# Rows of q and k copied by 0/1 matrices on TensorE instead of through DRAM, and two q projections moved into the attention groups

## The chip, the cores and the metric

One core of a Trainium2 chip runs one launch of the kernel. The metric is device time in microseconds (us). TensorE is called PE here, VectorE DVE, ScalarE ACT, GpSimd POOL; SP is the engine that only issues transfers.

## The reference

```python
x  = hidden_states                       # (4, 1024, 128), float32
xn = (x - mean(x)) / sqrt(var(x) + 1e-5)
q  = (xn @ Wq.T + bq).reshape(b, t, 16, 8)      # 16 heads of 8
k  = (xn @ Wk.T + bk).reshape(b, t, 4, 8)       # 4 key/value heads
v  = (xn @ Wv.T + bv).reshape(b, t, 4, 8)
q, k = q*cos + rotate_half(q)*sin, k*cos + rotate_half(k)*sin
scores  = einsum('bthd,bshd->btsh', q, repeat(k, 4)) / sqrt(8)
context = einsum('btsh,bshd->bthd', softmax(scores, axis=2), repeat(v, 4))
ffn = (silu(xn @ wg.T) * (xn @ wu.T)) @ wd.T    # 384 hidden, weights int * 1/127
out = x + context @ Wo.T + bo + ffn
```

## The kernel before

**Groups.** The attention is done in NG = 16 groups, one for each pair of batch and key/value head; a group has G = 4 query heads of 8 rows. Group g belongs to batch g // 4. Every group needs its q and k in an unusual shape: each float32 number is split in three bfloat16 parts (high, middle, low), and the six products of parts that matter (BLOCKS) are laid under one another, so that one matmul over 48 rows gives a score in nearly float32. In SBUF this is `qa`, `ka` (48 rows for even heads at rows 0 to 47, for odd heads at 64 to 111) and a second copy with three more rows for the maxima, `qc`, `kc`. So the same 8 rows of `part` (the tile of the three parts, q and k by row) must stand at several places of the partition axis.

**How the rows get there.** `part` is written to the DRAM tensors `q_rows`, `k_rows` (`store_k`, `store_q`, and a loop on POOL for group 0's q), and read back at the rows wanted (`load_k`, `load_q`, `load_parts`).

**Head.** x is loaded, each batch gets its moments (`moments`, DVE), the root and a Newton step (`root`, on ACT and on DVE), its normalised form `xn` (`normalise` on DVE for batch 0, on POOL for 1 and 2, by ACT for 3), its transposes (`transpose_xn` on PE, `copy_xn_T` on ACT). Batch 0's first 96 rows of q and its 32 rows of k are projected, rotated (`rotate`) and split on DVE and ACT. Then follow 48 units (LEAD) of the first group's row maxima, which this text calls the ramp.

**A unit.** `max_unit` on PE multiplies 128 queries with 512 keys (L916), DVE takes the maximum of the bank (`reduce_max`, L762). In the ramp the units go round three PSUM banks, and other work of PE is placed behind units by number: transposes of batches 2, 3 (PE_XN), the rest of k and q of batch 0 (PE_S1), v (PE_V, PE_VT), q of batches 2 and 3 (PE_Q, eight matmuls). `ident16`, and the weights of the feed-forward layer (`w_ffn`, L756), are converted on DVE ahead of the ramp. When the ramp is through, PE waits for `raw_done`, `w_done` and `qc_loaded`, and does the first four score matmuls (L933).

**Steps.** A group has 16 steps. In a step PE does four max units for a part of the rows that lies 48 units ahead, four score matmuls of the next step, at most one other job between them (JOB_AT, OUT_AT), and last `weigh` (L1002), which multiplies the exponentials with v. ACT makes the exponentials (L590), DVE the maxima. The units and the jobs of a step go round four PSUM banks in the order that `step_order` writes out; PE waits (`bank_left`) until the bank four places earlier has been read. Jobs GATE, UP at steps 1 to 4, 6, 7, NEG_T at 5 and 13, CTX at 8 and 16, DOWN at 10 and 11. Steps 9, 12, 14 and 15 have none in groups 0 and 1. Seven later groups have STAGE at 9 and PROJ at 12 and 14. A score matmul waits for the exponential three units back (`score_before`). After GATE, ACT makes two copies of its bank; after UP one.

**Later batches.** `split_later(b)` on POOL rotates and splits q of batch b, in group b - 1; it is followed by the stores to `q_rows`. Batch 1's q is projected just ahead of the ramp.

Of the kernel before, what the change touches and what calls it, by code (L numbers as in the profile page):

```python
# [67 lines left out]
MAX, GATE, UP, DOWN, NEG_T, CTX, STAGE, PROJ = "max", "gate", "up", "down", "neg_T", "ctx", "stage", "proj"  # L68

# [4 lines left out]
MIDDLE = (GATE, UP, DOWN, PROJ)  # L74
# [13 lines left out]
OUT_AT[NG - 1] = output_steps(OUTS - 2)  # L88

# [46 lines left out]
def attention_swiglu(nc, x, wf, wi, biases, bo, tables, identity, out):  # L136
# [3 lines left out]
    with ExitStack() as ctx:  # L140
# [11 lines left out]
        ident16 = sb("ident16", [P, P], BF16)  # L152
# [71 lines left out]


# [28 lines left out]
        q_first = sem("q_first")  # L254
# [6 lines left out]
        id_done = sem("id_done")  # L261
# [64 lines left out]
        def _(sp):  # L326
# [92 lines left out]
        def _(pool):  # L419
# [8 lines left out]
            for n, made in enumerate((part_hi, part_mid, part_lo)):  # L428
                pool.wait_ge(made, 2)
                for i, (_, c) in enumerate(BLOCKS):  # L430
                    if c == n:
                        pool.dma_start(q_rows[0:1, :, i, :, :].rearrange("g j d t -> (g j) d t"),
                                       part[0:G * HD, 0, n, :]).then_inc(q_first, 16)
            pool.wait_ge(rstd_done, 3)
            normalise(pool, nc.gpsimd, 2, xn_done_pool)

            def split_later(i):
# [3 lines left out]
                pool.wait_ge(raw_done, 2 * PROJECTED.index(i) + 2)  # L441
# [97 lines left out]
        def _(act):  # L539
# [4 lines left out]
            act.dma_start(bo_sb[:, :], bo.partition_broadcast(P)).then_inc(const_in, 16)  # L544
            act.dma_start(wi_sb[:, :], wi).then_inc(ffn_in, 16)
# [50 lines left out]
            split_high(0)  # L596
            split_high(1)
            split_mid(0)
            split_mid(1)
            copy_xn_T(1)  # L600
            act.wait_ge(const_in, 48)
            copy_later(1, 0)
            root(slice(2 * NT, NTT), 2 * NTT + 3)
            nc.scalar.preload_act_table(ACT.Exp)
            copy_later(1, 1)
            act.wait_ge(rstd_done, 3)
            for t in range(NT):
                n = (B - 1) * NT + t
                last = nc.scalar.activation(xn[:, B - 1, t, :], y_all[:, n, :], ACT.Identity,
                                            bias=shift[:, n:n + 1], scale=rstd[:, n:n + 1])  # L610
            last.then_inc(xn_done_act, 1)
            for b in range(2, B):
                copy_xn_T(b)
            for n in range(2):
                copy_later(0, n)
# [598 lines left out]
```

## Time and profile before

| | |
|---|---|
| time, median of 3 runs (lowest, highest) | 770.75 us (769.08, 771.15) |
| time of the profiled execution | 768.65 us |
| its span, first to last instruction | 766.0 us |
| PE busy | 720.9 us, 94% |
| DVE busy | 688.1 us, 90% |
| ACT busy | 621.9 us, 81% |
| POOL busy | 222.9 us, 29% |

2.65 us of the profiled execution lie outside its span. The head takes the first 34 us, the ramp lasts to about 69 us, the 16 groups to about 757 us. A time in a row is counted from the start of the span. A busy PE is not a PE at its peak, for its matmuls overlap; so the text goes by the distance between the starts of instructions.

### The profile page before, as it was taken

Reading aid. Unit: us, or ns where it says so; the run is one execution under the profiler, and the core shown is the slowest. Engines: PE = TensorE matmul, PEld = TensorE weight load, DVE = VectorE, ACT = ScalarE, POOL = GpSimd, SP = SyncE. Lnnn points to the kernel's source line nnn. Section 1 sums busy time; section 2 is a strip of 40 time slices with the busy share of each in tenths; the row PEclk is TensorE's granted clock in tenths of the full one; section 3 lists DMA queues with packets and bytes.
Section 4 is the critical chain, followed back from the end, with each engine's and each line's share of the span. In section 5 each row is a group of like instructions: output and inputs, shape, how many; then the busy total and the mean of one; then the engine's idle time right before and its main releaser. Section 6 shows DMA issues by size and latency. Waiting matters only on the chain.

```text
span 766.0 us, 13616 instructions
## 1 busy us (share of the span) xinstructions
PE 720.9 (94%) x4856; PEld 211.8 (28%) x4856; DVE 688.1 (90%) x1286; ACT 621.9 (81%) x1277; POOL 222.9 (29%) x364
## 2 busy tenths in 40 slices
PE   3598999999999999999999999999999999999997
PEld 1222222222222222323222222323222222323232
DVE  7688999999999999999999999999999999999911
ACT  1535989888888988888888978888897979888895
POOL 3408656473830302112030302112030302103030
PEclk9789999999999999999999999999999999999999
DMA  6511124031321101011111101011111101110020
GB/s 222 138 38 32 57 60 129 19 114 34 85 62 33 33 1 49 16 32 33 33 32 32 33 1 44 21 33 33 34 32 32 33 2 34 31 32 2 2 84 27
DMA packets 29450, 34.35 MB, mean 45 GB/s; under 512 B 5672, under 2 KB 20264, under 8 KB 29256
## 3 DMA queue, kind: packets, MB, share of 16 engines
q1 hardware_dynamic: 26600, 26.23, 12.5%
q0 software_dynamic: 1920, 5.12, 2.2%
q10 hardware_dynamic: 864, 2.15, 0.8%
q8 instruction: 38, 0.62, 0.3%
q14 instruction: 28, 0.23, 0.1%
HBM read 23.12 MB, written 9.96 MB: 43 GB/s over the span
## 4 chain that ended last, share of the span: by engine, by line
PE 74%; DVE 16%; ACT 5%; issue 2%; DMA 2%; SPq 1%; ACTq 0%; DVEq 0%
PE acc_ps L1002 29%; PE banks L916 19%; DVE mx L762 13%; PE banks L933 10%; PE banks L1007 8%; ACT probs L590 4%; PE banks L1021 3%; PE banks L1013 2%; PE banks L886 1%; PE banks L892 1%; PE banks L1056 1%; DMA k_rows<-part 1%; DMA y_all<-in_x 1%; DVE y_all L809 1%; PE banks L1029 1%
## 5 line engine op out<-in xcount | busy, mean ns | idle before, releaser
L762 DVE TENSOR_REDUCE mx<-banks 128x1 f32<-128x512 f32 x1024 | 639.2, 684 | 34.6 <-PE banks L916 32.0
L590 ACT ACTIVATE probs<-banks 128x512 f32<-128x512 f32 x1024 | 550.6, 605 | 95.0 <-PE banks L933 89.8
L933 PE MATMUL banks<-qc,kc 51*128 51x512 bf16 x1024 | 307.2, 383 | 10.8 <-ACT probs L590 7.1
L916 PE MATMUL banks<-ka,qa 48*128 48x512 bf16 x1024 | 302.7, 385 | 11.7 <-DVE mx L762 6.3
L1002 PE MATMUL acc_ps<-probs,v_grp 128*32 128x512 f32 x2048 | 273.4, 606 | 0.0
L916 PEld LDWEIGHTS banks<-ka,qa 48*128 48x128 bf16 x1024 | 67.8, 94 | 300.2 <-DVE mx L762 234.8
L471 POOL TENSOR_TENSOR neg_max<-row_max,nought 128x16 bf16<-128x16 f32 x31 | 6.8, 220 | 294.5 <-DVE row_max L768 294.5
L933 PEld LDWEIGHTS banks<-qc,kc 51*128 51x128 bf16 x1024 | 66.2, 94 | 46.6 <-ACT probs L590 43.3
L1007 PE MATMUL banks<-xn_T,w_ffn 128*128 128x256 f32 x192 | 67.1, 431 | 0.0
L1002 PEld LDWEIGHTS acc_ps<-probs,v_grp 128*32 128x32 f32 x2048 | 40.4, 108 | 82.1 <-ACT probs L590 54.5
L515 POOL TENSOR_TENSOR gated<-gu 128x256 f32<-128x256 f32 x48 | 35.1, 732 | 51.9 <-ACT gu L647 51.9
L486 POOL COPY v_grp<-v_all 128x64 f32<-128x64 f32 x16 | 3.7, 236 | 134.0 <-PE acc_ps L1002 99.6
L1007 PEld LDWEIGHTS banks<-xn_T,w_ffn 128*128 128x128 f32 x192 | 28.5, 188 | 40.1 <-DVE mx L762 26.0
L518 POOL TENSOR_TENSOR th<-th,gated 128x256 f32<-128x256 f32 x48 | 34.9, 726 | 3.8
L520 POOL TENSOR_TENSOR hid<-th,gated 128x256 f32<-128x256 f32 x48 | 34.8, 725 | 3.8
L1013 PE MATMUL banks<-w_ffn,hid 128*128 128x128 f32 x192 | 29.9, 292 | 0.0
L1013 PEld LDWEIGHTS banks<-w_ffn,hid 128*128 128x128 f32 x192 | 23.8, 190 | 13.2 <-issue 6.8
L1021 PE MATMUL banks<-ident,acc_sb 128*128 128x128 f32 x124 | 19.4, 279 | 2.1 <-ACT acc_sb L659 0.6
L886 PE MATMUL banks<-xn_T,wf_sb 128*128 128x512 f32 x32 | 19.6, 732 | 1.2 <-ACT xn_T L555 1.2
L644 ACT ACTIVATE gu<-banks 128x256 f32<-128x256 f32 x48 | 19.3, 403 | 0.0
L659 ACT ACTIVATE acc_sb<-acc_ps 128x512 f32<-128x512 f32 x31 | 18.6, 599 | 0.6
L647 ACT ACTIVATE gu<-banks 128x256 f32<-128x256 f32 x48 | 18.8, 391 | 0.0
(94 smaller groups left out, 314.3 us busy)
## 6 DMA issues: line engine op xcount, KB each, us to landing
qa<-q_rows SPq DMA_DIRECT2D x32, 192.0 KB, 3.4
qc<-q_rows SPq DMA_DIRECT2D x64, 96.0 KB, 2.6
q_rows<-part POOLq DMA_DIRECT2D x18, 256.0 KB, 4.3
ka<-k_rows SPq DMA_DIRECT2D x32, 96.0 KB, 2.2
kc<-k_rows SPq DMA_DIRECT2D x32, 96.0 KB, 2.2
y_all<-in_x SPq DMA_DIRECT2D x4, 512.0 KB, 9.7
out<-y_all SPq DMA_DIRECT2D x16, 128.0 KB, 2.0
k_rows<-part SPq DMA_DIRECT2D x6, 192.0 KB
```

Source lines behind the costliest of these rows:

```text
L515: nc.gpsimd.tensor_tensor(gated[:, c, :], gu[:, c, 0:CH], gu[:, c, CH:2 * CH], ALU.mult).then_inc(gated_done, 1)
L518: nc.gpsimd.tensor_tensor(th[:, c, :], th[:, c, :], gated[:, c, :], ALU.mult).then_inc(gated_done, 1)
L520: nc.gpsimd.tensor_tensor(hid[:, c, :], th[:, c, :], gated[:, c, :], ALU.add).then_inc(hid_done, 1)
L590: nc.scalar.activation(probs[:, s % SLOTS, j, :], banks[:, score_bank(G * s + j), :], ACT.Exp, scale=SCALE).then_inc(exp_done, 1)
L762: nc.vector.tensor_reduce(out=mx[:, h, col, k:k + 1], in_=ps, op=ALU.max, axis=AX.X).then_inc(max_done, 1)
L886: return nc.tensor.matmul(s_ps[:, n, h, :], wf_sb[:, c + n * D:c + (n + 1) * D], xn_T[:, b * T + h * W:b * T + (h + 1) * W], start=True, s ...
L916: nc.tensor.matmul(ps, qa[par][rows, j // 2, t * P:(t + 1) * P], ka[par][rows, k * W:(k + 1) * W], start=True, stop=True).then_inc(a_ready, 1)
L933: nc.tensor.matmul(banks[:, score_bank(u), :], kc[par][rows, kt * P:(kt + 1) * P], qc[par][rows, h, j // 2, :], start=True, stop=True).the ...
L1002: last = nc.tensor.matmul(acc_ps[VC * j:VC * (j + 1), :], v_grp[par][:, kt, :], probs[:, s % SLOTS, j, :], start=(kt == 0), stop=(kt == NT ...
L1007: nc.tensor.matmul(ps[:, 0:CH], w_ffn[:, n * HID + c * P:n * HID + (c + 1) * P], xn_T[:, g * CH:(g + 1) * CH], start=True, stop=True).then ...
L1013: last = nc.tensor.matmul(ps[:, 0:D], hid[:, c, t * P:(t + 1) * P], w_ffn[:, 2 * HID + c * D:2 * HID + (c + 1) * D], start=(c == 0), stop= ...
L1021: last = nc.tensor.transpose(ps[:, t * P:(t + 1) * P], acc_sb[:, h, t * P:(t + 1) * P], ident[:, :])
```

## The change

Group 0's `ka` and `qa` are no longer loaded from DRAM. A new input `select` holds seven 128x128 bfloat16 matrices, six of zeros and ones and the identity (it takes the place of `ident16`). For each half of the 1024 tokens `replicate` multiplies three of them per part (k, q of heads 0 and 1, q of heads 2 and 3) with the 32 rows of `part`, three parts added up in PSUM, and ACT copies six banks into `ka[0]` and `qa[0]` (`copy_rows`). `kc[0]` and `qc[0]` are then copied from those by six transfers inside SBUF. Other heads' rows go through DRAM as before, by SP alone.

The order of the head changes with it. On DVE `root` of batch 1 moves behind the rotation, the moments of batches 2 and 3 come between and behind the splits, `root` of batches 2 and 3 moves behind the first unit's maximum, and the conversion of `w_ffn` moves ahead of the maximum of unit 46. POOL normalises batches 1 and 3, ACT batch 2.

The projection of batch 1's q moves from ahead of the ramp into it (PE_Q, four matmuls), and that of batches 2 and 3 to steps 9, 12, 14 and 15 of groups 0 and 1: each such job, LATER_Q, is one matmul of 512 columns in float32 and one copy of its bank by ACT (`project_later`).

```diff
-PROJECTED = (1, 0, 2, 3)
-assert len(PROJECTED) == B
-PE_XN, PE_S1, PE_V, PE_VT, PE_Q = (3, 5, 7, 9), (11, 13, 15, 17), (19, 21), (23, 24), tuple(range(26, 42, 2))
+PROJECTED = (0, 1)
+PE_XN, PE_S1, PE_V, PE_VT, PE_Q = (8, 10, 12, 14), (16, 18, 20, 22), (24, 26), (28, 29), (31, 35, 37, 39)
...
+for g in range(B - 2):
+    OUT_AT[g] = {9: (LATER_Q, 0), 12: (LATER_Q, 1), 14: (LATER_Q, 2), 15: (LATER_Q, 3)}
...
+        def select_bank(i):
+            return banks[:, (6, 4, 5, 1, 2, 3)[i], :]
...
-                store_k(slice(0, KV), slice(Q_ROWS, P), 0, n, k_stored[0])
+                store_k(slice(1, KV), slice(Q_ROWS + HD, P), 0, n, k_stored[0])
+                store_q(slice(1, KV - 1), slice(G * HD, Q_ROWS), 0, n, q_stored_too[0])
+            sp.wait_ge(ones_set, 4)
+            sp.wait_ge(select_done, 2 * PARTS)
+            for e in range(2):
+                rows = slice(e * E_ROWS, e * E_ROWS + MAX_ROW)
+                sp.dma_start(kc[0][rows, :], ka[0][rows, :]).then_inc(qc_loaded[0], 16)
+                for h in range(NH):
+                    sp.dma_start(qc[0][rows, h, :, :], qa[0][rows, :, h * W:(h + 1) * W]).then_inc(qc_loaded[0], 16)
             sp.wait_ge(k_stored[0], BLOCK_DMAS)
-            load_k(0, ka[0], qa_loaded[0])
-            sp.wait_ge(q_first, BLOCK_DMAS)
-            load_q(0, qa[0], qa_loaded[0])
-            sp.wait_ge(ones_set, 4)
-            load_parts(0, qc[0], kc[0], qc_loaded[0])
-            for n in range(PARTS):
-                store_q(slice(1, KV - 1), slice(G * HD, Q_ROWS), 0, n, q_stored_too[0])
...
-            for n, made in enumerate((part_hi, part_mid, part_lo)):
-                pool.wait_ge(made, 2)
-                for i, (_, c) in enumerate(BLOCKS):
-                    if c == n:
-                        pool.dma_start(q_rows[0:1, :, i, :, :].rearrange("g j d t -> (g j) d t"),
-                                       part[0:G * HD, 0, n, :]).then_inc(q_first, 16)
             pool.wait_ge(rstd_done, 3)
-            normalise(pool, nc.gpsimd, 2, xn_done_pool)
+            normalise(pool, nc.gpsimd, B - 1, xn_done_pool)
...
+                    pool.wait_ge(raw_later, 2 * NH * (i - 1))
...
+            act.dma_start(select_sb[:, :], select.bitcast(BF16)).then_inc(select_in, 16)
...
+            def copy_rows(i, rows):
+                act.wait_ge(select_ps, i + 1)
+                nc.scalar.activation(rows, select_bank(i), ACT.Copy).then_inc(select_done, 1)
+            def project_later(b, i, ps):
+                n, h = divmod(i, NH)
+                act.wait_ge(q_ps, 2 * len(PROJECTED) + 2 * NH * (b - 2) + i + 1)
+                nc.scalar.activation(raw[b][:, n, HALF[h]], ps, ACT.Identity,
+                                     bias=bias_sb[:, B_Q + n:B_Q + n + 1]).then_inc(raw_later, 1)
...
+            split_mid(0)
+            copy_rows(0, ka[0][:, HALF[0]])
             split_high(1)
-            split_mid(0)
+            copy_rows(1, qa[0][:, 0, HALF[0]])
             split_mid(1)
+            copy_rows(2, qa[0][:, 1, HALF[0]])
+            copy_rows(3, ka[0][:, HALF[1]])
+            for i in range(PAIRS):
+                copy_rows(4 + i, qa[0][:, i, HALF[1]])
             copy_xn_T(1)
-            act.wait_ge(const_in, 48)
-            copy_later(1, 0)
             root(slice(2 * NT, NTT), 2 * NTT + 3)
             nc.scalar.preload_act_table(ACT.Exp)
-            copy_later(1, 1)
             act.wait_ge(rstd_done, 3)
             for t in range(NT):
-                n = (B - 1) * NT + t
-                last = nc.scalar.activation(xn[:, B - 1, t, :], y_all[:, n, :], ACT.Identity,
+                n = 2 * NT + t
...
-            for i in PROJECTED[2:]:
-                for n in range(2):
-                    if (i, n) == (PROJECTED[-1], 0):
-                        copy_neg(0, 0, first_bank(NEG_BEHIND + 1))
-                    copy_later(i, n)
+            copy_neg(0, 0, first_bank(NEG_BEHIND + 1))
+            for n in range(2):
+                copy_later(1, n)
...
-            root(slice(NT, 2 * NT), 1)
...
+            rotate(0, 0)
+            rotate(0, 1)
+            rope_half(0)
+            rotate(1, 0)
+            rest_of_high(0)
+            rotate(1, 1)
+            low(0)
+            rope_half(1)
+            root(slice(NT, 2 * NT), 1)
+            rest_of_high(1)
+            moments(2, 4 * NT + 2)
+            low(1)
+            moments(3, 6 * NT + 2)
             add_eps(slice(2 * NT, NTT), 2 * NTT + 2)
-            root(slice(2 * NT, NTT), 2)
-            nc.vector.tensor_copy(ident16[:, :], ident[:, :]).then_inc(id_done, 1)
-            dve.wait_ge(ffn_in, 16)
-            for n, scale in ((slice(0, 2 * HID), DEQUANT), (slice(2 * HID, 3 * HID), 0.5 * DEQUANT)):
-                nc.vector.tensor_scalar(w_ffn[:, n], wi_sb[:, n], scale, None, ALU.mult).then_inc(w_done, 1)
             def reduce_max(g, a, ps):
                 dve.wait_ge(a_ready, AU * g + a + 1)
@@ -794,6 +828,12 @@
                 made.then_inc(neg_step, 1)
             for a in range(LEAD):
+                if a == 1:
+                    root(slice(2 * NT, NTT), 2)
+                if a == LEAD - 2:
+                    dve.wait_ge(ffn_in, 16)
+                    for n, scale in ((slice(0, 2 * HID), DEQUANT), (slice(2 * HID, 3 * HID), 0.5 * DEQUANT)):
...
+            def replicate(h, n, made):
+                pe.wait_ge(made, h + 1)
+                k_rows, q_rows = slice(Q_ROWS, P), slice(0, G * HD)
+                for i, (rows, a) in enumerate(((k_rows, 0), (q_rows, 0), (q_rows, 1))):
+                    c = (PARTS * a + n) * P
+                    last = nc.tensor.matmul(select_bank(3 * h + i), select_sb[rows, c:c + P], part[rows, 0, n, HALF[h]],
+                                            start=(n == 0), stop=(n == PARTS - 1))
+                    if n == PARTS - 1:
+                        last.then_inc(select_ps, 1)
+            pe.wait_ge(select_in, 16)
+            for h in range(2):
+                if h == 1:
+                    pe.wait_ge(rope_mul, 2 * NH)
+                for n, made in enumerate((part_hi, part_mid, part_lo)):
+                    replicate(h, n, made)
             for h in range(2):
                 transpose_xn(1, h)
-            pe.wait_ge(xnt_done, 4)
-            for n in range(2):
-                pe.wait_ge(rope_mul, 3 + n)
-                for h in range(2):
-                    last = project(C_Q, 1, n, h)
-                last.then_inc(q_ps, 1)
...
-            pe.wait_ge(qa_loaded[0], DMAS)
             for a in range(LEAD):
+                if a in (0, 2, 4):
+                    pe.wait_ge(select_done, 2 + a // 2)
...
-                    b, n, h = 2 + PE_Q.index(a) // 4, PE_Q.index(a) // 2 % 2, PE_Q.index(a) % 2
-                    if h == 0:
-                        if b > 2:
-                            pe.wait_ge(raw_done, 2 * (b - 1) + n + 1)
-                        elif n == 1:
-                            pe.wait_ge(v_done, 1)
-                    last = project(C_Q, b, n, h)
+                    n, h = divmod(PE_Q.index(a), NH)
+                    if n == 1 and h == 0:
+                        pe.wait_ge(v_done, 1)
+                    last = project(C_Q, 1, n, h)
...
+            def project_later(b, i, ps):
+                n, h = divmod(i, NH)
+                nc.tensor.matmul(ps, wf_sb[:, C_Q + n * D:C_Q + (n + 1) * D],
+                                 xn_T[:, b * T + h * W:b * T + (h + 1) * W], start=True, stop=True).then_inc(q_ps, 1)
...
+    for i, parts in enumerate(BLOCKS):
+        for e, d in itertools.product(range(2), range(HD)):
+            column = e * E_ROWS + i * HD + d
+            select[Q_ROWS + d, parts[0], column] = one
+            for pair in range(PAIRS):
+                select[(2 * pair + e) * HD + d, PARTS * pair + parts[1], column] = one
```

## Rows read from the trace of the kernel before

**Rows 1.** Chain that ended last, in order of time: start us, length us, what.

```profile
23.61 4.71 DMA k_rows<-part
...
29.68 3.60 DMA qa<-q_rows
```

**Rows 2.** Timeline of the head: start us, length us, engine, line, what, idle before.

```profile
15.51 4.92 POOL L315 TENSOR_SCALAR xn<-y_all,rstd,shift 128x128 f32<-128x128 f32 x8 [10.82 <-DVE shift L714]
...
16.83 0.69 DVE L737 TENSOR_TENSOR ctx_all<-probs 128x512 f32<-128x512 f32 x1
...
17.55 0.63 ACT L560 ACTIVATE part<-ctx_all 128x512 bf16<-128x512 f32 x1 [3.40 <-DVE ctx_all L737]
...
19.51 0.68 DVE L742 TENSOR_TENSOR ctx_all<-ctx_all,part 128x512 f32<-128x512 f32 x1
...
22.42 1.64 DVE L691 BATCH_NORM_STATS2 stats<-y_all 128x6 f32<-128x128 f32 x8
...
24.66 1.61 DVE L691 BATCH_NORM_STATS2 stats<-y_all 128x6 f32<-128x128 f32 x8
...
27.66 0.25 DVE L704 RECIPROCAL rc<-sd 128x16 f32<-128x16 f32 x1 [0.50 <-ACT sd L550]
...
29.01 0.82 DVE L756 TENSOR_SCALAR w_ffn<-wi_sb 128x768 f32<-128x768 int32 x2
...
29.07 4.00 POOL L315 TENSOR_SCALAR xn<-y_all,rstd,shift 128x128 f32<-128x128 f32 x8 [4.83 <-DVE shift L714]
```

**Rows 3.** Timeline of the ramp, same columns.

```profile
33.97 2.48 DVE L762 TENSOR_REDUCE mx<-banks 128x1 f32<-128x512 f32 x4 [4.14 <-PE banks L916]
...
35.25 1.12 PE L880 MATMUL banks<-ident,xn 128*128 128x128 f32 x4
...
40.12 1.29 DVE L762 TENSOR_REDUCE mx<-banks 128x1 f32<-128x512 f32 x2 [0.30 <-PE banks L916]
...
43.81 7.88 DVE L762 TENSOR_REDUCE mx<-banks 128x1 f32<-128x512 f32 x12 [0.82 <-PE banks L916]
...
53.09 1.12 PE L886 MATMUL banks<-xn_T,wf_sb 128*128 128x512 f32 x2
...
53.20 4.83 DVE L762 TENSOR_REDUCE mx<-banks 128x1 f32<-128x512 f32 x7 [0.21 <-PE banks L916]
...
61.73 8.41 DVE L762 TENSOR_REDUCE mx<-banks 128x1 f32<-128x512 f32 x13 [0.66 <-PE banks L916]
...
68.62 0.60 PE L933 MATMUL banks<-qc,kc 51*128 51x512 bf16 x3
```

**Rows 4.** Windows of time, all engines; the clock column is the last but two.

```profile
40.00:42.00 2.00, 1.85 (x12) 1.00 (x14) 1.58 (x3) 0.78 (x2) 0.00 (x0) 0.50 0.65 154
...
44.00:48.00 4.00, 4.00 (x34) 0.76 (x30) 3.91 (x7) 1.64 (x2) 0.00 (x0) 1.00 0.02 4
```

**Rows 5.** Timeline of PE, the matmuls that end steps 2, 3, 8, 9, 11 to 15 of group 0.

```profile
78.47 1.06 PE L1002 MATMUL acc_ps<-probs,v_grp 128*32 128x512 f32 x8
81.18 1.06 PE L1002 MATMUL acc_ps<-probs,v_grp 128*32 128x512 f32 x8
...
94.53 1.06 PE L1002 MATMUL acc_ps<-probs,v_grp 128*32 128x512 f32 x8
97.02 1.07 PE L1002 MATMUL acc_ps<-probs,v_grp 128*32 128x512 f32 x8
...
102.90 1.06 PE L1002 MATMUL acc_ps<-probs,v_grp 128*32 128x512 f32 x8
105.38 1.06 PE L1002 MATMUL acc_ps<-probs,v_grp 128*32 128x512 f32 x8
107.87 1.07 PE L1002 MATMUL acc_ps<-probs,v_grp 128*32 128x512 f32 x8
110.84 1.06 PE L1002 MATMUL acc_ps<-probs,v_grp 128*32 128x512 f32 x8
113.33 1.07 PE L1002 MATMUL acc_ps<-probs,v_grp 128*32 128x512 f32 x8
```

More of the change, by code:

```diff
@@ L1 @@
+import itertools
 from contextlib import ExitStack
@@ L72 @@
           10: (DOWN, 0), 11: (DOWN, 1), 13: (NEG_T, 0), 16: (CTX, 1)}
-MIDDLE = (GATE, UP, DOWN, PROJ)
+MIDDLE = (GATE, UP, DOWN, PROJ, LATER_Q)
 OUTS = 2 * B
@@ L133, in score_before, with attention_swiglu @@
     return max(v for v in range(-SG, u) if score_bank(v % SG) == score_bank(u))
-def attention_swiglu(nc, x, wf, wi, biases, bo, tables, identity, out):
+def attention_swiglu(nc, x, wf, wi, biases, bo, tables, identity, select, out):
     q_rows = nc.dram_tensor("q_rows", (NG, G, len(BLOCKS), HD, T), BF16, kind="Internal").ap()
@@ L260, in attention_swiglu @@
         w_done = sem("w_done")
-        id_done = sem("id_done")
+        select_in = sem("select_in")
+        select_ps = sem("select_ps")
+        select_done = sem("select_done")
         bo_added = sem("bo_added")
@@ L440, in split_later @@
                 rows, twin = (raw[i][:, k, :] for k in range(2))
-                pool.wait_ge(raw_done, 2 * PROJECTED.index(i) + 2)
+                if i in PROJECTED:
+                    pool.wait_ge(raw_done, 2 * i + 2)
+                else:
+                    pool.wait_ge(raw_later, 2 * NH * (i - 1))
                 nc.gpsimd.tensor_tensor(rows, rows, rope[:, 0, :], ALU.mult).then_inc(q_step, 1)
@@ L648, in group @@
                                                  ACT.Copy).then_inc(gu_done, 1)
+                        if kind == LATER_Q:
+                            project_later(g + 2, n, bank(slot))
                         if kind == NEG_T:
@@ L730, in _, with rope_half @@
             add_eps(slice(NT, 2 * NT), 4 * NT + 1)
-            root(slice(NT, 2 * NT), 1)
             dve.wait_ge(const_in, 48)
-            for h in range(2):
-                rotate(h, 0)
-                rotate(h, 1)
+            def rope_half(h):
                 dve.wait_ge(rope_mul, 2 * (h + 1))
@@ L738, in _, with rest_of_high @@
                     .then_inc(rope_sum, 1)
-            for h in range(2):
+            def rest_of_high(h):
                 dve.wait_ge(rope_sum, h + 1)
@@ L743, in _, with low @@
                                         ALU.subtract).then_inc(part_res, 1)
-            for h in range(2):
+            def low(h):
                 dve.wait_ge(part_res, h + 1)
@@ L748, in _ @@
                                         ALU.subtract).then_inc(part_lo, 1)
-            for b in range(2, B):
-                moments(b, 2 * b * NT + 2)
-            add_eps(slice(2 * NT, NTT), 2 * NTT + 2)
-            root(slice(2 * NT, NTT), 2)
-            nc.vector.tensor_copy(ident16[:, :], ident[:, :]).then_inc(id_done, 1)
-            dve.wait_ge(ffn_in, 16)
-            for n, scale in ((slice(0, 2 * HID), DEQUANT), (slice(2 * HID, 3 * HID), 0.5 * DEQUANT)):
-                nc.vector.tensor_scalar(w_ffn[:, n], wi_sb[:, n], scale, None, ALU.mult).then_inc(w_done, 1)
+            rotate(0, 0)
[11 more added lines that the diff above has]
+            moments(3, 6 * NT + 2)
+            add_eps(slice(2 * NT, NTT), 2 * NTT + 2)
             def reduce_max(g, a, ps):
@@ L876, in transpose_xn @@
                     pe.wait_ge(xnt_done, 2 * b + h - 1)
-                if b == 2 and h == 0:
-                    pe.wait_ge(raw_done, 1)
                 for t in range(HT):
@@ L901, in _ @@
                     project(C_S0, 0, n, h).then_inc(proj_ps, 1)
+            def replicate(h, n, made):
[13 more added lines that the diff above has]
+                    replicate(h, n, made)
             for h in range(2):
                 transpose_xn(1, h)
-            pe.wait_ge(xnt_done, 4)
-            for n in range(2):
-                pe.wait_ge(rope_mul, 3 + n)
-                for h in range(2):
-                    last = project(C_Q, 1, n, h)
-                last.then_inc(q_ps, 1)
             def max_unit(par, a, ps):
@@ L1069, in bank_left @@
                     pe.wait_ge(y_done, CT * g + n + 1)
+                elif kind == LATER_Q:
+                    pe.wait_ge(raw_later, 2 * NH * g + n + 1)
                 elif kind == NEG_T:
@@ L1098, in take @@
                     ffn_down_proj(g, n, ps)
+                elif kind == LATER_Q:
+                    project_later(g + 2, n, ps)
                 elif kind == NEG_T:
@@ L1168, in _ @@
                 group(g, g // 2, g % 2, min(3, NG - g))
-_INS = ["x", "wf", "wi", "biases", "bo", "tables", "identity"]
+_INS = ["x", "wf", "wi", "biases", "bo", "tables", "identity", "select"]
 def kernel(**inputs):
@@ L1201 @@
     tables = np.stack([cos, sin], axis=1).astype(np.float32)
+    one = np.uint16(0x3F80)
+    select = np.zeros((P, PAIRS * PARTS + 1, P), dtype=np.uint16)
+    for i, parts in enumerate(BLOCKS):
[4 more added lines that the diff above has]
+                select[(2 * pair + e) * HD + d, PARTS * pair + parts[1], column] = one
+    select[range(P), PAIRS * PARTS, range(P)] = one
     arrays = {
@@ L1205 @@
         "identity": np.eye(P, dtype=np.float32),
+        "select": select.reshape(P, -1),
     }
```

30 lines of the change are left out of this document (17 added, 13 removed).

## The prediction

> **What bounds the kernel now.** I read the chain that ended last first. In the head it runs through two transfers, the store of k's parts to DRAM and the load of q from it [rows 1]; these the change takes off. Behind them it goes through PE, DVE and ACT by turns, with no transfer. Next the timeline of the head, for what stands ready when the transfers are gone; of the ramp, for what paces a unit; of PE in one group, for what a step costs with and without a job; and the windows, for the clock.
>
> The head: the first maximum begins at 33.97 after 4.14 us of idle DVE [rows 3]. So up to 4.1 us of pure waiting are to be had, and more only if DVE's work ahead of it shrinks.
>
> The ramp: alone, units come every 0.62 us (2.48 for 4); with a q projection behind every second one, every 0.69 us (4.83 for 7) [rows 3]. PE sets that pace, so each projection costs 2 x 0.07 = 0.14 us.
>
> A step: a step with no job (9, 12) takes 2.49 us, one with GATE or UP (3) 2.71 [rows 5]. In the latter PE is the limit. In the former it isn't: the fourth score matmul waits for the first exponential, and four maxima at 0.62 take 2.49 as well.
>
> **The head, worked out.** The first half's rotated rows stand at 16.83 + 0.69 = 17.52 as before [rows 2]. DVE then does, in the new order, a `rotate` of about 0.7 (18.2), `rest_of_high(0)` 0.68 (18.9; ACT's high part is ready, 17.55 + 0.63), `rotate` (19.6), `low(0)` (20.3), `rope_half(1)` (21.0) and `root` of batch 1. The like `root` took from 27.66 to just before the conversion at 29.01, with a small cast in it [rows 2]: 1.2 for its six instructions, so 22.2. From there three lines run:
> - DVE: `rest_of_high(1)` 22.9; moments of batch 2, 2.24 (22.42 to 24.66 [rows 2]), 25.15; `low(1)` 25.85; moments of batch 3, 28.1; eps 28.3.
> - POOL: `xn` of batch 1, 4.00 to 4.92 [rows 2], so 26.2 to 27.2. PE's eight transposes follow in two bursts of 1.12 that overlap a little [rows 3]: 28.1 to 29.1. Before, this root came at 14 and POOL began at 15.51; this is what is late next.
> - PE and ACT: the 18 select matmuls (512 columns each) are nowhere in the trace. Bounds: nothing, hidden behind DVE's splits, or, at the low clock, three of 0.43 each behind the last split. The last three banks can be copied from 25.85 + 0.6 = 26.5, 0.6 each (ACT's 512 columns take 0.63 [rows 2]): 28.4. Then two copies of `xn_T` behind the transposes to 29.7, and the square root to 29.9.
>
> So PE does unit 0 at 28.1 to 29.1 and DVE begins it at 28.7 to 29.6, 5 us earlier than now. But behind it stands `root` of batches 2 and 3, 1.2 us, which waits for ACT's square root: it ends at 31.1 to 31.5. I take 31.4 for the start of unit 1's maximum, against 33.97 + 0.62 = 34.6: **-3.2**. A dozen hand-overs between engines, at some 0.05 each, could add 0.6.
>
> **The ramp.** Four q projections instead of eight: 4 x 0.14 = **-0.55** (bounds 0 and -0.6). The other bursts are the same ones, five units later, and batches 2 and 3 stand normalised by 31.5 + 4 = 35.5, about when unit 8 is due. At the end the conversion of `w_ffn`, 0.82 [rows 2], which lay in the idle time ahead of the ramp, stands ahead of unit 46's maximum, and PE waits for it before the first scores. Now: unit 47's maximum ends at 61.73 + 8.41 = 70.14, so unit 44's at 68.2, and the scores start 0.4 later, at 68.62 [rows 3]. After: unit 44's ends at 68.2 - 3.2 - 0.55 = 64.45, unit 45's at 65.1, the conversion at 65.9, scores at about 65.95. That is **-2.65** for everything behind. In SP's queue twelve stores, six copies inside SBUF and group 1's loads stand ahead; from 22.2 on they have 40 us until the scores need `qc`, and so cost nothing; with no such cover each would add its issue. POOL loses six issues ahead of the second normalisation, which waits for `root` anyway. The `select` load has from about 4 to 18 us.
>
> **The moved projections.** Eight jobs of 512 columns, against 256 for GATE. In float32 such a matmul stands as two records; for 512 columns the two last 1.12 with the latency at their end [rows 3], of which 0.85 are streaming (1024 columns at two cycles each and 2.4 GHz). GATE's 256 columns stream for half of that, so the longer job adds 0.43 to a step like GATE's: LATER_Q step = 2.71 + 0.43, about 3.13. The bounds are the row's whole 1.12 on top of a step of 2.49, with no slack used (3.61, excluded as far as GATE's step shows that slack is used), and 3.13. ACT's copy of 0.6 is hidden: GATE steps carry two copies. The ring: four more slots per group, a multiple of its four banks, so nothing else changes its bank.
> - Step 9: 97.02 - 94.53 = 2.49 becomes 3.13, +0.64. Step 12 (102.90 to 105.38) +0.65. Step 15 (110.84 to 113.33) +0.64.
> - Step 13 (2.49): DVE has caught up in step 12, so it may give back up to 0.16.
> - Step 14 is 2.97 already (107.87 to 110.84), as the last score matmul of a group waits for the second exponential, not the first. The job lies in that wait: +0.16.
>
> Sum 1.9 to 2.1 per group, for two groups **+4.0** (bounds +3.2, if twice as much comes back, and +4.6, if step 14 pays in full as well).
>
> **Sum.** 766.0 - 2.65 + 4.0 = 767.35 span, 770.0 with the 2.65 outside it. The profiled execution lay 2.1 below the median of the runs, so the median goes from 770.75 to **772.1**, +0.17%. About 0.3% (2.3 us) is what a measurement of this kernel can tell from no change.
>
> **Rivals.**
> - *The clock (ends slower).* PE ran at the low level, 1.2 GHz, from the ramp's start to 42 and at 2.4 GHz from 44 [rows 4]; there the first burst of L892 left DVE idle for 0.82 and each of the transposes' four for about 0.3 [rows 3]. Now eight bare units come first and the bursts five units later, in sparser work. If the low level lasts through the three other bursts of PE_S1, each costs 0.82: +2.5, so 774.6. It decides from two bursts on (772.1 + 1.6 = 773.7). Against: the bursts themselves are the same that brought the clock up before. The Trainium skill ("TensorE: Matmul & The Clock Gate", Part 1, What's actually happening) says that the array's default is the throttled state and activity releases it; by that rule the sparser start is for this rival, and the row at 40 to 42 agrees.
> - *The head gives more (ends faster).* If unit 1's maximum waits for nothing but DVE's queue (28.3, unit 0, 1.2 of root: 30.1), the clock is high in the ramp (those gaps, 0.82 and four of 0.3, are gone) and the moved jobs cost their lower bound: 772.1 - 1.3 - 2.0 - 0.8 = 768.0. The one mechanism is the clock again, the other way: select matmuls and transposes directly ahead of the ramp, where PE now idles. It decides if it takes both the gaps and at least one us of the head.
> - *The jobs hide.* The steps of no job have slack of 0.42 each on PE; if the ring carried it over whole groups, 4 x 0.42 and step 14's wait would pay for more and the jobs would cost 1.0 less per group: 770.1, no change. Against: the ring is four banks deep, not a step.
> - *The head gives less.* If `xn` of batch 1 or the hand-overs cost 1.5 more, 773.6, slower.
>
> **Chances.** Forecast 0.40 (own range 770.8 to 773.4), clock 0.20, head less 0.13, head more 0.15, jobs hide 0.12. From these: faster by over 0.3% 0.15, within it 0.50 (part of the forecast's own spread passes the bound), slower 0.35. Range 768.9 to 775.0: it reaches to the clock's rival and to where the faster one begins.
>
> **What would show it.** First max unit at 28 to 29, `root` between the maxima of units 0 and 1, unit 1's maximum near 31.4; first scores near 66; a PE wait for `w_ffn` ahead of them; steps 9, 12, 15 of groups 0 and 1 at 3.13, step 14 at 3.1; group 2 on as before, the whole later by 1.3. Wrong would be: jobs of under 0.4 us, bursts of L892 with gaps of 0.8 after 45, or a first unit after 30.

## The result, and the profile after

In the runs made together, six of each kernel, before had a median of 769.3 us and the changed kernel 775.33 (772.21 to 778.73). The ratio is 1.0075, with a 95% interval from 1.0057 to 1.0093: slower by 0.75%, where 772.1 and no change that can be told were forecast, and above the range, which ended at 775.0.

The profiled execution shown here is the slowest of the six, 778.73 us with a span of 776.9. So its figures overstate the median's loss: 10.9 us of span against before's 766.0, where the medians lie 6.0 apart. First the head and the ramp, in the timeline (start, length, engine, line, what, idle before):

```profile
22.20 4.34 POOL L329 TENSOR_SCALAR xn<-y_all,rstd,shift 128x128 f32<-128x128 f32 x8 [17.51 <-DVE shift L741]
...
28.71 1.03 PE L965 MATMUL banks<-ka,qa 48*128 48x512 bf16 x3
...
29.35 0.69 DVE L796 TENSOR_REDUCE mx<-banks 128x1 f32<-128x512 f32 x1 [1.12 <-PE banks L965]
...
31.17 4.87 DVE L796 TENSOR_REDUCE mx<-banks 128x1 f32<-128x512 f32 x8
...
43.41 7.88 DVE L796 TENSOR_REDUCE mx<-banks 128x1 f32<-128x512 f32 x12 [0.84 <-PE banks L965]
...
57.13 2.07 PE L924 MATMUL banks<-xn_T,wf_sb 128*128 128x512 f32 x2
...
59.78 1.29 DVE L796 TENSOR_REDUCE mx<-banks 128x1 f32<-128x512 f32 x2 [1.85 <-PE banks L965]
...
62.33 1.29 DVE L796 TENSOR_REDUCE mx<-banks 128x1 f32<-128x512 f32 x2 [1.26 <-PE banks L965]
...
66.97 2.12 POOL L470 TENSOR_TENSOR part<-raw,part 128x1024 bf16<-128x1024 f32 x1
67.74 4.19 DVE L836 TENSOR_SCALAR w_ffn<-wi_sb 128x768 f32<-128x768 int32 x2
69.17 4.95 POOL L509 TENSOR_TENSOR y_all<-y_all,bo_sb 128x1024 f32<-128x1024 f32 x2
71.84 1.28 DVE L796 TENSOR_REDUCE mx<-banks 128x1 f32<-128x512 f32 x2
...
72.03 1.01 PE L982 MATMUL banks<-qc,kc 51*128 51x512 bf16 x3 [4.14 <-DVE w_ffn L836]
```

The head came as worked out. `xn` of batch 1 took 4.34, unit 0 was multiplied at 28.71, the maximum of unit 1 began at 31.17 (31.4 was forecast), 3.4 us ahead of before [rows 3]. Then the lead is lost. Two things stand out: the conversion of `w_ffn` takes 4.19 us instead of 0.82 [rows 2], while POOL works before it, beside it and behind it, and PE stands idle for 4.14 until it is done; and the q projections at 57.13 last 2.07 instead of the 1.12 of [rows 3], with DVE idle for 1.85 and 1.26. The first scores start at 72.03, 3.4 late against 68.62 and 6.1 after the forecast.

The windows of the same execution, whose third column from the end is the granted clock:

```profile
44.00:56.00 12.00, 9.46 (x62) 2.64 (x59) 10.66 (x22) 4.61 (x5) 0.98 (x3) 1.00 0.00 0
56.00:64.00 8.00, 7.79 (x15) 2.01 (x15) 4.41 (x7) 1.31 (x3) 7.78 (x5) 0.57 0.25 75
64.00:72.00 8.00, 2.68 (x8) 0.48 (x6) 7.86 (x9) 0.94 (x1) 7.78 (x5) 0.66 0.00 1
72.00:84.00 12.00, 11.63 (x44) 2.37 (x44) 6.91 (x12) 7.38 (x16) 6.74 (x3) 0.52 0.01 2
```

Before had 1.00, 1.00, 0.90 and 0.93 in these four. Now the clock is at its low level, 1.2 GHz, for most of 56 to 84. From 44 to 56 PE is busy for 9.46 us instead of 11.09, from 64 to 72 for 2.68 instead of 6.42.

What PE did just before the clock fell stands in its timeline. One matmul of a unit lasts 0.39 at the high level and 0.60 at the low one:

```profile
55.49 0.23 PE L970 MATMUL banks<-select_sb,neg_max 128*96 128x128 bf16 x1 [1.35 <-DVE neg_max L827]
56.00 0.39 PE L965 MATMUL banks<-ka,qa 48*128 48x512 bf16 x1 [0.28 <-DVE mx L796]
56.60 0.60 PE L965 MATMUL banks<-ka,qa 48*128 48x512 bf16 x1 [0.21 <-DVE mx L796]
...
66.68 1.20 PE L965 MATMUL banks<-ka,qa 48*128 48x512 bf16 x2 [0.21 <-DVE mx L796]
```

The first fall, between the units at 56.00 and 56.60, comes behind a wait of 1.35 us for the maxima that PE has to transpose (`neg_max`), with bare units (units with no other work of PE behind them) on its other side. The second is there by 66.68, behind bare units and ahead of the conversion (67.74): PE's long stop did not cause that fall, it lies inside the low stretch. Before has the same wait for `neg_max`, shorter and with a q projection directly behind the next unit, and its clock stays high there:

```profile
59.43 0.23 PE L921 MATMUL banks<-ident,neg_max 128*96 128x128 bf16 x1 [0.76 <-DVE neg_max L793]
59.94 0.39 PE L916 MATMUL banks<-ka,qa 48*128 48x512 bf16 x1 [0.28 <-DVE mx L762]
60.25 1.12 PE L886 MATMUL banks<-xn_T,wf_sb 128*128 128x512 f32 x2
```

Last comes PE's timeline at the ends of steps 0 to 2, 8, 9 and 11 to 15 of group 0, as in [rows 5]:

```profile
75.38 1.94 PE L1047 MATMUL acc_ps<-probs,v_grp 128*32 128x512 f32 x8
80.76 1.94 PE L1047 MATMUL acc_ps<-probs,v_grp 128*32 128x512 f32 x8
84.77 1.07 PE L1047 MATMUL acc_ps<-probs,v_grp 128*32 128x512 f32 x8
...
100.83 1.07 PE L1047 MATMUL acc_ps<-probs,v_grp 128*32 128x512 f32 x8
103.96 1.06 PE L1047 MATMUL acc_ps<-probs,v_grp 128*32 128x512 f32 x8
...
109.84 1.06 PE L1047 MATMUL acc_ps<-probs,v_grp 128*32 128x512 f32 x8
112.97 1.06 PE L1047 MATMUL acc_ps<-probs,v_grp 128*32 128x512 f32 x8
115.46 1.06 PE L1047 MATMUL acc_ps<-probs,v_grp 128*32 128x512 f32 x8
118.59 1.07 PE L1047 MATMUL acc_ps<-probs,v_grp 128*32 128x512 f32 x8
121.79 1.07 PE L1047 MATMUL acc_ps<-probs,v_grp 128*32 128x512 f32 x8
```

Step 9 takes 3.13, step 12 3.13, step 13 2.49, step 14 3.13 and step 15 3.20: 0.64, 0.65, 0, 0.16 and 0.71 more than in [rows 5], 2.16 in the group.

The budget of this execution against before's: 3.4 us later at the first scores, 6.3 at the end of step 2 (84.77 against 78.47), still 6.3 at the end of step 8, 8.5 behind step 15, 2.16 more in group 1, 0.3 elsewhere; 10.9 in all.

The six runs of the changed kernel say how much of this varies. From the longest to the shortest, with the mean granted clock of each:

```
778.73 us  0.971
776.24 us  0.975
775.82 us  0.976
774.84 us  0.978
773.92 us  0.978
772.21 us  0.980
```

A faster run never has a lower clock. From 0.980 to 0.971 is 0.009 x 777 x 2 = 14 us more at the low level, and 6.5 us more time.

### The profile page after: what moved, and what is told of

Its sections match the earlier page's. It is cut to its first block, busy times and chain, and to the rows that moved or that the text cites. A ratio compares the mean times of both kernels' runs of the same rounds, so it can differ in the third digit from the quotient of the medians.

```text
span 776.9 us, 13656 instructions
## 1 busy us (share of the span) xinstructions
PE 731.5 (94%) x4874; PEld 212.1 (27%) x4874; DVE 692.2 (89%) x1285; ACT 626.1 (81%) x1287; POOL 218.5 (28%) x358
## 4 chain that ended last, share of the span: by engine, by line
PE 78%; DVE 15%; ACT 4%; issue 2%; DMA 1%; SPq 0%; ACTq 0%; DVEq 0%
PE acc_ps L1047 29%; PE banks L965 20%; DVE mx L796 12%; PE banks L982 11%; PE banks L1057 8%; ACT probs L613 3%; PE banks L1071 3%; PE banks L1063 2%; PE banks L924 1%; PE banks L1053 1%; PE banks L930 1%; PE banks L1106 1%; DMA y_all<-in_x 1%; PE banks L918 1%; DVE w_ffn L836 1%
## 5 line engine op out<-in xcount | busy, mean ns | idle before, releaser
L965 PE MATMUL banks<-ka,qa 48*128 48x512 bf16 x1024 | 308.2, 389 | 8.2 <-DVE mx L796 8.2
L667 ACT ACTIVATE th<-banks 128x256 f32<-128x256 f32 x48 | 18.8, 392 | 0.8 <-PE banks L1057 0.8
```

Of the source, the lines that this page charges most:

```text
L965: nc.tensor.matmul(ps, qa[par][rows, j // 2, t * P:(t + 1) * P], ka[par][rows, k * W:(k + 1) * W], start=True, stop=True).then_inc(a_ready, 1)
```

## The experiments

Two theories stood to be tested. **P**: an instruction of DVE that converts from SBUF to SBUF stands still while POOL has an instruction running, and at unit 46 POOL does. **C**: the sparser ramp and PE's stop let the clock fall, and the bursts (the projections behind a unit) and first steps then run at the low level. Rivals: **L**, the conversion is slow for itself in that place; **W**, the clock only goes with waits that would be there anyway. Each ratio is to the kernel before, run in turn on the same chip; the changed kernel's is 1.0075.

**conv10.** The conversion ahead of unit 10's maximum.

```diff
-                if a == LEAD - 2:
+                if a == 10:
                     dve.wait_ge(ffn_in, 16)
```

> The changed kernel with one piece moved: the conversion of w_ffn on DVE stands ahead of unit 10's maximum instead of unit 46's, where POOL is idle. Theory P (the conversion took 4.19 us at unit 46 because an instruction of POOL was running, and PE stood still behind it for 4.14 us, which also let the clock fall): the conversion takes about 0.82 again, the first scores start near 67.5 instead of 72.03, and the low clock of 17 us around there shrinks to some 3 to 7 us. Time 5 to 8 us below the changed kernel's 775.3, so 767.5 to 770.5. Theory L (the conversion is slow for itself wherever it stands in the ramp): it still takes 4 us, now in front of unit 10, and the time stays within 2 us of 775.

Measured: 772.7, ratio 1.0034 (1.0017 to 1.0051), better than the changed kernel's 1.0075, whose interval begins at 1.0057, just above this one's end. The conversion in DVE's timeline:

```profile
36.10 0.82 DVE L836 TENSOR_SCALAR w_ffn<-wi_sb 128x768 f32<-128x768 int32 x2
```

0.82, so L falls. The first scores start at 65.48 in this execution; 1.0 us of that lead stands already at the first maximum (28.32 against 29.35), which the edit does not touch. But the clock was still 0.67 in the window from 56 to 64 and 0.57 in the next, and the gaps of 1.85 and 1.26 are still there: moving the conversion does not mend the clock in the ramp. The gain is 2.6 us by medians, 3.2 by ratios, where 5 to 8 were expected.

**poolheld.** The conversion stays at unit 46, POOL waits for it.

```diff
                 pool.wait_ge(q_step, n + 5)
+                if i == 0:
+                    pool.wait_ge(w_done, 2)
                 nc.gpsimd.tensor_copy(part[:, slot, 1, :], twin).then_inc(q_step, 1)
```

> The changed kernel with one wait more: POOL holds the last two instructions of the split of batch 0's q, and what follows, until w_ffn is converted; the conversion stays at unit 46. Theory P: with POOL idle the conversion takes 0.82 us instead of 4.19, the first scores start near 68.6, 3.4 us earlier than 72.03, and the low clock behind it is shorter; time 771 or less. Theory L: the conversion takes about 4.2 us as before and the time stays near 775.

Measured: 772.27, ratio 1.0043 (1.0021 to 1.0066). DVE's and POOL's timelines:

```profile
68.11 0.82 DVE L838 TENSOR_SCALAR w_ffn<-wi_sb 128x768 f32<-128x768 int32 x2
```

```profile
63.93 2.12 POOL L466 TENSOR_TENSOR raw<-raw,part 128x1024 f32<-128x1024 f32 x1
69.06 1.04 POOL L470 CAST part<-raw 128x1024 bf16<-128x1024 f32 x1 [3.02 <-DVE w_ffn L838]
```

In the same place, with POOL idle, it takes 0.82. This settles what P says of the duration. The time is less sure: 3.1 us better by medians, but the interval overlaps the changed kernel's (from 1.0057), and the median misses the 771 expected. In this execution PE's wait ahead of the scores is down to 0.77, and the clock is still low, 0.69 from 64 to 72 and 0.64 from 72 to 84.

**before_conv46.** The kernel before, with the conversion at unit 46 (the same lines, moved).

> The kernel before with one piece moved: the conversion of w_ffn from ahead of the ramp to ahead of unit 46's maximum. Theory P: POOL works there in this kernel too, so the conversion's two instructions take 2.5 to 4.5 us, PE waits for them before the first scores, and the clock falls for longer than the 3.4 us of before: 773 to 777 against 769.3. Theory L's variant (the delay belongs to the other changes of the head): 0.8 us and at most 771.

Measured: 773.16, ratio 1.005 (1.0031 to 1.0069). The two timelines:

```profile
71.14 2.40 DVE L797 TENSOR_SCALAR w_ffn<-wi_sb 128x768 f32<-128x768 int32 x2
```

```profile
69.89 2.12 POOL L454 TENSOR_TENSOR raw<-raw,part 128x1024 f32<-128x1024 f32 x1
72.07 1.25 POOL L456 CAST part<-raw 128x1024 bf16<-128x1024 f32 x1
```

2.40, with ends that go with POOL's: the first of its two instructions lasts 1.29 instead of 0.55 and ends 0.41 behind POOL's first row, the second lasts 1.19 instead of 0.35 and ends 0.21 behind POOL's cast, which itself takes 1.25 instead of 1.04. One misplaced instruction pair alone makes the kernel before 0.5% slower (four runs), more than its own 1.6 us; the rest was not taken apart.

**before_laterq.** The kernel before with the moved projections of batches 2 and 3 alone.

```diff
-PROJECTED = (1, 0, 2, 3)
+PROJECTED = (1, 0)
...
-PE_XN, PE_S1, PE_V, PE_VT, PE_Q = (3, 5, 7, 9), (11, 13, 15, 17), (19, 21), (23, 24), tuple(range(26, 42, 2))
+PE_XN, PE_S1, PE_V, PE_VT, PE_Q = (3, 5, 7, 9), (11, 13, 15, 17), (19, 21), (23, 24), ()
...
+for g in range(B - 2):
+    OUT_AT[g] = {9: (LATER_Q, 0), 12: (LATER_Q, 1), 14: (LATER_Q, 2), 15: (LATER_Q, 3)}
```

> The kernel before with q of batches 2 and 3 projected at steps 9, 12, 14, 15 of groups 0 and 1 alone (the ramp then holds no q projection). The step theory: each of the two groups is longer by 2.16 us (0.64, 0.65, 0.16, 0.71), the ramp shorter by 8 x 0.14 = 1.1. If that is all: 769.3 + 4.3 - 1.1 = 772.5. Theory C (the bursts of the ramp also kept the clock up): without them the low level returns before unit 47 and lasts into the first steps, 2 to 4 us more: 774.5 to 776.5.

Measured: 773.42, ratio 1.0056 (1.004 to 1.0071). Its windows:

```profile
56.00:64.00 8.00, 6.09 (x13) 1.17 (x12) 7.42 (x17) 0.27 (x1) 4.18 (x2) 0.50 0.08 20
64.00:72.00 8.00, 7.66 (x22) 1.66 (x25) 6.87 (x12) 2.89 (x7) 7.63 (x6) 0.50 0.20 56
```

Without the q bursts the clock is low from 56 to 72, and the weigh of step 0 takes 1.94. The steps cost what they cost in the change (98.53 - 95.40 = 3.13 for step 9). Without the clock 772.5 was expected, with it 774.5 to 776.5: the time lies between, so it decides for neither, and what shows the clock's part here is the windows (before had 1.00 and 0.90).

**conv10_fill.** conv10 with 16 idle matmuls on PE (their result is read by nobody), 13 behind units and three ahead of the wait for `neg_max`.

```diff
+FILL = (30, 32, 33, 34, 36) + tuple(range(40, 48))
...
+            def fill(n):
+                for _ in range(n):
+                    nc.tensor.matmul(acc_ps[:, :], select_sb[:, 0:P], select_sb[:, 0:W], start=True, stop=True)
...
+                if a in FILL:
+                    fill(1)
                 if a == NEG_BEHIND:
+                    fill(3)
```

> The kernel of conv10 (the change with the conversion of w_ffn at unit 10) with 16 idle bf16 matmuls of 512 columns added on PE, in the stretches of the ramp where it does bare units (units 30, 32 to 34, 36, 40 to 47) and three ahead of the wait for the maxima's transposition; they write a bank that nobody reads, and at the high clock they fit beside DVE's 0.62 us a unit. Theory C (the low clock in the second half of the ramp and the first steps comes from PE's sparse work there, as batches 2 and 3 of q have left): the clock stays high or comes back sooner, the gaps of 1.85, 1.26 and 0.68 us before the maxima of units 35 to 40 and the slow first steps go: 3 to 5 us faster than conv10, near 768 against before's 769.1, so faster than or equal to before. Rival W (the time is in the waits themselves, the clock only goes with them): no faster than conv10, or slower by up to 3 us as the added matmuls take PE time.

Measured: 768.37, ratio 1.0003 (0.9988 to 1.0019), against conv10's 1.0034 (1.0017 to 1.0051). conv10's window from 56 to 64 first, then this one's:

```profile
56.00:64.00 8.00, 7.08 (x15) 1.50 (x13) 4.45 (x8) 2.23 (x2) 7.71 (x5) 0.67 0.28 75
```

```profile
56.00:64.00 8.00, 8.00 (x23) 2.10 (x22) 6.54 (x11) 2.23 (x2) 7.78 (x5) 1.00 0.24 75
```

More work on PE, and DVE does 11 instructions instead of 8 in the same 8 us. The two intervals against before overlap by 0.0002; by medians the gain is 4.3 us, by means 2.5, and 8 of its 12 runs lie under 769 against one of 12 of conv10's. This is the change with both faults mended, and it is no faster than before.

**before_fill.** The kernel before with idle matmuls at units 33, 34 and 41 to 47, and three ahead of the wait for `neg_max`.

> The kernel before with idle matmuls on PE at units 33, 34, 41 to 47 and three ahead of the wait for the maxima's transposition. Theory C: the 3.4 us of low clock at 70.3 go, and with them the first weigh at 1.93 instead of 1.06: 0.5 to 1.5 us faster than before. Without it: no change, or slower by under 1 us.

Measured: 770.04, ratio 1.0011 (0.9998 to 1.0024): nothing gained. The clock was low for a while behind 70 in this execution too (the weigh of step 0 took 1.93). Idle matmuls are no sure means; here they didn't keep the clock from falling at the first scores.

**q2ramp.** conv10, with q of batch 2 in the ramp again and batch 3's alone left to the steps of group 1.

```diff
-PE_XN, PE_S1, PE_V, PE_VT, PE_Q = (8, 10, 12, 14), (16, 18, 20, 22), (24, 26), (28, 29), (31, 35, 37, 39)
+PE_XN, PE_S1, PE_V, PE_VT, PE_Q = (8, 10, 12, 14), (16, 18, 20, 22), (24, 26), (28, 29), (30, 31, 35, 37, 39, 41, 43, 45)
...
-for g in range(B - 2):
+for g in (1,):
```

> The kernel of conv10 with q of batch 2 projected in the ramp again (PE_Q is 30, 31, 35, 37, 39, 41, 43, 45, for batches 1 and 2); only batch 3's q is left to the steps, of group 1. The step theory: group 0 takes its 43.0 again, -2.16; four bursts more in the ramp, +0.55; and by theory C the denser ramp keeps the clock up, -1 to -3. Sum 2.5 to 4.5 below conv10's 772.7, so 768 to 770. Without theory C 1.6 below: 771.

Measured: 768.21, ratio 0.9997 (0.9977 to 1.0016), 0.37% under conv10's: the time is as expected. The reason given for a part of it is not: with eight bursts in the ramp again the clock still fell at the same place, as PE's timeline and DVE's show.

```profile
54.91 0.23 PE L972 MATMUL banks<-select_sb,neg_max 128*96 128x128 bf16 x1 [0.75 <-DVE neg_max L829]
55.42 0.39 PE L967 MATMUL banks<-ka,qa 48*128 48x512 bf16 x1 [0.28 <-DVE mx L798]
56.02 0.60 PE L967 MATMUL banks<-ka,qa 48*128 48x512 bf16 x1 [0.21 <-DVE mx L798]
```

```profile
59.20 1.29 DVE L798 TENSOR_REDUCE mx<-banks 128x1 f32<-128x512 f32 x2 [1.85 <-PE banks L967]
```

Its bursts at 30 and 31 stand ahead of the wait for `neg_max`, and units 32 to 34 are as bare as in the change. The granted clock is 0.58 from 56 to 64, and 1.00 from 64 on.

**q2ramp_fill.** The same with idle matmuls at units 32, 33, 34, 36, 46, 47.

> The kernel of q2ramp with idle matmuls on PE at units 32, 33, 34, 36, 46, 47 and three ahead of the wait for the maxima's transposition. If both theories hold it is the fastest of these: 765.5 to 768. If the clock is not it: as q2ramp.

Measured: 769.43, ratio 0.9997 (0.9983 to 1.0011): no gain. The expectation that it would be the fastest was wrong. The idle matmuls did what they were put in for: 1.00 from 56 to 64, where q2ramp had 0.58. But the clock was low in the first steps in this execution (the weigh of step 0 took 1.94), and it came up later, 0.52 from 36 to 44 against 0.83; the mean clock of both executions is 0.984. So a held clock in one stretch does not by itself make the run shorter.

**new_head_only.** The new head alone: 0/1 matrices and new order, conversion at unit 10, batch 1's q behind units 1 to 4, no projection in the steps.

```diff
-PE_XN, PE_S1, PE_V, PE_VT, PE_Q = (8, 10, 12, 14), (16, 18, 20, 22), (24, 26), (28, 29), (31, 35, 37, 39)
+PE_XN, PE_S1, PE_V, PE_VT, PE_Q = (9, 11, 13, 15), (17, 19, 21, 23), (25, 27), (29, 30), (31, 32, 35, 37, 39, 41, 43, 45)
+Q1_AT = (1, 2, 3, 4)
...
-for g in range(B - 2):
-    OUT_AT[g] = {9: (LATER_Q, 0), 12: (LATER_Q, 1), 14: (LATER_Q, 2), 15: (LATER_Q, 3)}
```

> The changed kernel without its moved projections: the 0/1 matrices and the new order of the head stay, the conversion of w_ffn is at unit 10, q of batch 1 is projected behind units 1 to 4 (where PE waits while DVE does the root of batches 2 and 3), the transposes and what follows one unit later, q of batches 2 and 3 in the ramp as before the change (31, 32, 35, 37, 39, 41, 43, 45); no job in steps 9, 12, 14, 15 of groups 0 and 1. The step theory: 4.3 below conv10 (772.7), plus 4 x 0.14 for the four bursts and 0 to 3 for batch 1's q at the low clock: 768.5 to 771.5. Theory C adds: a busy PE from 29 on and a dense end of the ramp bring the high clock sooner and hold it, -1 to -3: 766 to 769, that is 0 to 0.4% faster than before's 769.2. Rival (the new head alone gives nothing, because DVE's work ahead of unit 1 is the same): no faster than before, 769 or more.

Measured: 770.29, ratio 1.0016 (1.0001 to 1.003). No faster than before. With the next version beside it the reason can be told in part, below.

**new_head_spread.** The same with `Q1_AT = (1, 2, 5, 7)`.

> As new_head_only, with q of batch 1 behind units 1, 2, 5 and 7 instead of 1 to 4. If PE's low clock is what costs there, spreading gives DVE's maxima time to go on: up to 1 us faster; if density raises the clock sooner, up to 1 us slower.

Measured: 766.27, ratio 0.9962 (0.9948 to 0.9976): 0.38% faster than before (six runs); this version and the next are the only ones here that are faster than both kernels clear of noise. Its first scores and first two weighs in PE's timeline, then the weighs of the kernel before:

```profile
68.08 0.60 PE L984 MATMUL banks<-qc,kc 51*128 51x512 bf16 x3 [0.88 <-ACT raw L579]
...
71.02 1.07 PE L1060 MATMUL acc_ps<-probs,v_grp 128*32 128x512 f32 x8
74.11 1.06 PE L1060 MATMUL acc_ps<-probs,v_grp 128*32 128x512 f32 x8
```

```profile
71.78 1.93 PE L1002 MATMUL acc_ps<-probs,v_grp 128*32 128x512 f32 x8
...
75.77 1.07 PE L1002 MATMUL acc_ps<-probs,v_grp 128*32 128x512 f32 x8
```

The scores start only 0.5 us sooner than in before, but the two weighs stand at 71.02 and 74.11 instead of 71.78 and 75.77, as both run at the high clock. Of the 2.0 us between these two executions, then, most is the clock at this joint, not the head.

It is 4.0 us better than new_head_only, where 1 us was expected. The runs split that: new_head_only's three runs with a mean clock of 0.989, the clock of all six here, took 767.9 to 768.24, so at the same mean clock some 1.8 us are left, and the rest is its nine runs at 0.980 to 0.987. The profiles of the two differ by 2.1 us (spans of 764.0 and 766.1). Of these 0.96 stands already at the first maximum (29.50 against 28.54), which the edit does not touch. Behind it the four projections in a row are no loss: new_head_only needs 0.8 less up to the conversion at unit 10. It loses 1.9 between its starts at 40.8 and 47.8, where its clock is down again (0.53 from 40 to 47, against 1.00).

**spread_conv46.** That kernel with the conversion back at unit 46.

> The kernel of new_head_spread (0.4% faster than before) with the conversion of w_ffn moved back from unit 10 to unit 46 and nothing else. Theory P: POOL is busy there again, the two instructions take 2.4 to 4.5 us, PE waits, and the clock may fall behind it. Of that, about 1.7 lies beside the wait for the last copy of q (0.88 of PE's idle time) and the units' own pace; 2 to 5 us slower than new_head_spread: 768.5 to 771.5, ratio to before 1.000 to 1.003. If the port does not matter in this place: ratio 0.996 to 0.997.

Measured: 767.14, ratio 0.9969 (0.9957 to 0.9982): slower than new_head_spread by 0.9 us by medians, with overlapping intervals, and not by 2 to 5. The conversion in DVE's timeline:

```profile
65.77 1.94 DVE L836 TENSOR_SCALAR w_ffn<-wi_sb 128x768 f32<-128x768 int32 x2
```

It took 1.94, as its first instruction met the end of one of POOL's (64.06 to 66.18) and its second a cast of 1.25. Of the 1.91 us that PE stood idle ahead of the scores, 0.88 are there without it. The same line in the same place costs 4.19, 2.40 or 1.94, by where POOL stands.

## Why the prediction was wrong

The steps that held: the order of the head and its times (unit 0's matmul between 28 and 29, `root` between the first two maxima, unit 1's at 31.17 for 31.4); the job's price (3.13 in steps 9 and 12, as said, 3.13 for 14); PE's wait for `w_ffn` ahead of the scores was foreseen, its length was not. The bursts of L892 (now L930) had one gap of 0.84, as before, and none after 45: the clock rival did not come about in the place where I put it, and that the median lies near its 774.6 is luck. Small misses: step 13 gave nothing back and step 15 cost 0.71, so 4.3 for two groups where 4.0 stood.

The step that failed first is the sentence that the conversion costs "0.82 [rows 2]" in its new place. I took its duration from a row in which POOL was idle until 0.06 us after it had begun, and moved it 38.7 us on, to unit 46, without asking what POOL does there. It took 4.19. Even in that row POOL's first instruction, begun 0.06 us behind the conversion, lasted 1.00 us and its next ones 0.44: there POOL stood still for DVE. Theory P is shown: 0.82 with POOL held, 0.82 where POOL is idle, 2.40 in the kernel before with nothing else changed. The Trainium skill ("SBUF — State Buffer", SBUF: two separate sides) has it as a rule: VectorE and GpSimd share a pair of SBUF ports under an exclusive lock, held for a whole instruction, so of a VectorE operation that uses both port pairs and one of GpSimd the later waits for the earlier. The trace agrees: the two instructions lasted 1.77 and 2.49 us, the first until 69.51, 0.42 behind the end of POOL's (66.97 + 2.12 = 69.09), the second until 71.92, 0.21 behind the end of POOL's next one (71.71), which took 2.53 instead of 2.12 itself. In before_conv46 and spread_conv46 the two distances are 0.41 or 0.42 and 0.21 or 0.22. The maxima around it, which read PSUM, kept their 0.68 beside POOL's work. No run here shows the ports themselves, only the waiting.

The step that failed second is the sum's silence on the clock behind unit 30. The rival asked only whether the bursts at units 16 to 22 would run slow. With fewer bursts in the second half PE was busy for 9.46 of 12 us instead of 11.09, the clock fell near 56, the bursts of units 35 and 37 then cost 1.85 and 1.26 of DVE's time instead of 0.14, and the low level that began again ahead of PE's stop of 4.14 lasted into the first steps, until 84. The number of bursts alone doesn't decide: q2ramp has eight, and its clock fell behind the same wait for `neg_max`, with units 32 to 34 as bare. The versions with something for PE there kept 1.00 from 56 to 64: new_head_only and new_head_spread with a burst at unit 32, conv10_fill and q2ramp_fill with idle matmuls. No run moves one burst alone, so this is what goes together with the fall, not a shown cause of it.

Against the forecast of -2.65 at the first scores the profile has +3.4. Of these 6.1 us, 4.19 - 0.82 = 3.4 are the conversion and some 2.8 the slow bursts; another 2.9 us are lost between the first scores and the end of step 2 (84.77 - 72.03 = 12.7 against 78.47 - 68.62 = 9.9).

That the clock itself is the cause, not a companion of the waits, rests on conv10_fill (4.3 us by medians) and on the six runs of one kernel, whose times go with their clocks; against it stands q2ramp_fill, which held the clock from 56 to 64 and gained nothing. How much of the median's 6.0 us is the clock's can't be split exactly, as it differs from run to run: conv10, 1.0034, has the conversion's share taken off (0.4%, with what it did to the clock), conv10_fill, 1.0003, what idle matmuls give back of the clock (0.3%), and what is left is the head's gain against 4.3 us of steps.

That the six copies inside SBUF and SP's longer queue cost nothing is only argued: no wait in the head or at the scores was put down to them. The select matmuls may cost a little: in the changed kernel the transposes behind the last three began at 26.81, 0.27 after POOL's `xn` was done (22.20 + 4.34 = 26.54).

## What to carry to other kernels

When an instruction that only had to be done "sometime" is moved, look up what each other engine does in its new place, not only whether its own engine has room: a conversion on DVE has a different price beside POOL's work. When work leaves a stretch of PE, ask what holds the clock there, above all beside a wait of PE's own; a burst that costs 0.14 us at 2.4 GHz can cost 1.85 at 1.2. And a job put into steps of a loop that PE nearly fills costs there what the loop's slack doesn't cover (0.64 of 1.06 us), while behind every second unit of the ramp it cost 0.14.

## What was not expected of the hardware

DVE's conversion from int32 to float32, 0.82 us for both instructions, took 4.19, 2.40 and 1.94 beside POOL, and POOL's instructions grew beside it in turn (1.00 for 0.44, 2.53 for 2.12). One and the same program varies by 6.5 us (772.21 to 778.73), with mean granted clocks of 0.980 and 0.971. The clock fell behind waits of PE of 1.35 and 0.75 us with bare units around them. And idle matmuls helped in one kernel (conv10_fill, 1.00 from 56 to 64) and gave no time in two others, though in one of these the clock was 1.00 in the same stretch.
